# One Trainium2 core, attention plus routed experts: how the expert tokens reach TensorE transposed

## The reference

```
x + attention(xn) + experts(xn)
logits = xn @ gate_w.T ; probs = softmax(logits) over 8 experts ; two best experts a token
h = gelu(w1[e] @ xn + b1[e])            # 512 hidden features
y = w2[e] @ h + b2[e]                   # 128 features
experts(xn) = sum over the two choices of prob * y
```

## Time and profile before

| | us |
|---|---|
| three runs | 724.34, 726.56, 726.74 (median 726.56) |
| span of the profiled execution, first to last instruction | 724.1 |
| the profiled execution's own time beside its span | none is given by the profile |
| PE / DVE / ACT / POOL busy | 663.7 / 650.1 / 531.9 / 514.5 |
| expert stage, first product of tile 2 to that of tile 70 | 307.45 to 502.62 |

### The profile page before, as it was taken

How to read it: one execution, slowest core, us unless ns; L and a number is a source line. 1 busy time by engine, 2 the same in 40 slices (tenths; PEclk the granted TensorE clock), 3 DMA queues, 4 the chain that set the end, 5 groups by cost and what they waited for, 6 DMA issues and landing times.

```text
span 724.1 us, 25378 instructions
## 1 busy us (share of the span) xinstructions
PE 663.7 (92%) x8084; PEld 448.1 (62%) x8084; DVE 650.1 (90%) x1177; ACT 531.9 (73%) x1123; POOL 514.5 (71%) x613
## 2 busy tenths in 40 slices
PE   0377899999999999799999999999999999999996
PEld 0263445555555555599999999999455555555554
DVE  8989989999999999699999999999899999898991
ACT  2593388888888888667767767777787787787885
POOL 8680477777677656077777887787688888888782
PEclk9986799999999999999999999999999999999999
DMA  8859466776676676633333333332577777877652
GB/s 249 307 170 336 135 166 169 182 200 161 175 209 173 174 191 174 160 76 96 93 96 93 97 96 90 97 92 75 142 155 179 191 178 183 173 178 187 176 122 67
DMA packets 124919, 113.37 MB, mean 157 GB/s; under 512 B 16416, under 2 KB 112416, under 8 KB 124832
## 3 DMA queue, kind: packets, MB, share of 16 engines
q1 hardware_dynamic: 115600, 90.63, 47.7%
q0 software_dynamic: 8192, 16.86, 9.6%
q10 hardware_dynamic: 1040, 4.76, 1.8%
HBM read 64.72 MB, written 47.19 MB: 155 GB/s over the span
## 4 chain that ended last, share of the span: by engine, by line
PE 65%; DVE 13%; SPq 8%; DMA 6%; issue 5%; ACT 2%; ACTq 0%; DVEq 0%
PE bank L1266 13%; PE mx L1255 13%; PE bank L1135 12%; PE bank L1113 11%; PE mx L1147 7%; DVE mx L961 6%; DMA stack<-qk_dram 6%; PE bank L1033 2%; PE bank L1247 2%; PE bank L1195 2%; DVE A L796 2%; SPq L331 2%; PE bank L1157 1%; ACT A L715 1%; PE bank L1164 1%
## 5 line engine op out<-in xcount | busy, mean ns | idle before, releaser
L715 ACT ACTIVATE A<-bank 128x512 f32<-128x512 f32 x502 | 278.2, 597 | 63.8 <-PE bank L1135 55.8
L961 DVE TENSOR_REDUCE mx<-mx 128x4 f16<-128x1024 f32 x256 | 302.7, 1205 | 19.1 <-PE mx L1147 14.7
L1135 PE MATMUL bank<-stack 113*128 113x256 f16 x1004 | 170.4, 276 | 1.3 <-ACT A L715 0.8
L761 ACT ACTIVATE rows<-mx,b 128x256 f32<-128x256 f32 x284 | 120.1, 480 | 57.7 <-PE mx L1255 55.3
L556 POOL DMA_INDIRECT slots_x<-rows,pos x128 | 123.6, 966 | 51.8 <-PE bank L1135 32.0
L570 POOL TENSOR_SCALAR rows<-rows,slot_p 128x128 f32<-128x128 f32 x142 | 124.6, 887 | 43.9 <-DVE rows L1009 43.9
L607 POOL DMA_INDIRECT rows<-slots_y,pos x128 | 121.5, 950 | 37.5 <-issue 17.3
L1113 PE MATMUL bank<-A,V 128*32 128x256 f32 x2048 | 137.9, 387 | 1.7 <-ACT A L715 1.6
L1135 PEld LDWEIGHTS bank<-stack 113*128 113x128 f16 x1004 | 72.4, 97 | 89.4 <-ACT A L715 53.8
L1266 PE MATMUL bank<-w,rows 128*128 x1704 | 107.7, 219 | 0.6 <-DVE rows L1003 0.6
L1003 DVE TENSOR_TENSOR rows<-rows 128x512 f16<-128x512 f32 x142 | 101.4, 714 | 4.9
(11 more groups left out here) (145 smaller groups left out, 684.9 us busy)
## 6 DMA issues: line engine op xcount, KB each, us to landing
stack<-ctx_rest SPq DMA_DIRECT2D x64, 256.0 KB
stack<-qk_dram SPq DMA_DIRECT2D x128, 96.0 KB
rows<-slots_x SPq DMA_DIRECT2D x71, 129.0 KB, 2.3
slots_y<-rows SPq DMA_DIRECT2D x71, 128.0 KB, 1.8
qk_dram<-hi_qk SPq DMA_DIRECT2D x64, 128.0 KB
stack<-ctx_high SPq DMA_DIRECT2D x128, 64.0 KB
slots_x<-A ACTq DMA_DIRECT2D x1, 4644.0 KB, 20.3
w_stage<-in_w SPq DMA_DIRECT2D x8, 512.0 KB
```

Of the source, the lines that this page charges most:

```text
L715: act.activation(A[:, n % NA, :, :].rearrange("p h s -> p (h s)"), scores(k, n)[:, :], ACT.Exp, scale=SCALE).then_inc(s_xp, 1)
L761: act.activation(h32[r % 2][:, fc, :], bank[fc][:, 0:SLOT], ACT.Gelu_apprx_tanh, bias=b1[:, bass.ds(e + fc, 1)], scale=1 / FS).then_inc(s_ ...
L961: dve.tensor_reduce(mx[:, a, 8 * qt:8 * qt + 8].rearrange("q (i e w) -> q i e w", i=2, e=2)[:, :, g % 2], MX[u % 2][:, :].rearrange("q (i ...
L1135: mm = pe.matmul(scores(k, n)[:, i * S:(i + 1) * S], stack[0:SHIFT + 1, par, h, 1, c * P:(c + 1) * P], stack[0:SHIFT + 1, par, h, 0, :], s ...
```

## The change

It changes how a tile's tokens get from `slots_x` to TensorE and divides the two casts of the hidden values.

- `fetch(n)` is now two transfers on SP's queue: a transposing transfer of columns 2 to 257 of the tile's 256 rows straight into `xt[n % 4]`, and a small one of the first float32 of each row into `slot_p`. `xt` has four buffers, the raw buffers `xr` are gone. For n >= 4 both wait until all four groups of w1 of tile n-4 are done and until POOL has multiplied tile n-4.
- PE has no transposes in the stage, ACT no `turned_tokens`, POOL no copy of the probabilities. w1(t) waits for the transposing transfer of tile t.
- The cast of the hidden chunks 2 and 3 moves from DVE to ACT, behind the fourth Gelu of the same tile, whose completion it waits for. DVE's second subtraction waits for it (`s_fa`).

```diff
@@ buffers
-        xr32 = [carve(RW, F32).rearrange("p (s c) -> p s c", s=2) for _ in range(4)]
-        xr = [v.bitcast(F16) for v in xr32]
-        xt = [carve(2 * SLOT, F16).rearrange("p (a s) -> p a s", a=2) for _ in range(2)]
+        xt = [carve(2 * SLOT, F16).rearrange("p (a s) -> p a s", a=2) for _ in range(4)]
@@ SP
-            xs = slots_x.rearrange("(n s p) c -> n p s c", s=2, p=P)
+            xs = slots_x.bitcast(F16).rearrange("(n s) c -> n s c", s=SLOT)
+            ps = slots_x.rearrange("(n s p) c -> n p s c", s=2, p=P)
...
                 if n >= 4:
-                    sp.wait_ge(s_ft, n - 3)
-                    sp.wait_ge(s_sp, n - 3)
-                sp.dma_start(xr32[n % 4], xs[n]).then_inc(s_xr[n % 4], 16)
+                    sp.wait_ge(s_fu, 4 * (n - 3))
+                    sp.wait_ge(s_yp, n - 3)
+                sp.dma_start_transpose(xt[n % 4], xs[n][:, 2:RW]).then_inc(s_xr[n % 4], 16)
+                sp.dma_start(slot_p[:, n % 4, :].unsqueeze(2), ps[n][:, :, 0:1], allow_slow_non_contiguous=True).then_inc(s_sp[n % 4], 16)
@@ POOL
-                pool.wait_ge(s_sp, n + 1)
+                pool.wait_ge(s_sp[n % 4], 16 * (n // 4 + 1))
                 pool.wait_ge(s_fy, n + 1)
...
             for n in range(ET):
-                pool.wait_ge(s_xr[n % 4], 16 * (n // 4 + 1))
-                if n >= 4:
-                    pool.wait_ge(s_yp, n - 3)
-                pool.tensor_copy(slot_p[:, n % 4, :], xr32[n % 4][:, :, 0]).then_inc(s_sp, 1)
-                if n >= 3:
-                    weigh(n - 3)
-            for n in range(ET - 3, ET):
                 weigh(n)
@@ ACT
-            def turned_tokens(n):
-
-                act.wait_ge(s_ft, n + 1)
-                if n >= 2:
-                    act.wait_ge(s_fu, 4 * n - 4)
-                act.activation(xt[n % 2].rearrange("p a s -> p (a s)"), bank[4 + n % 2][:, 0:SLOT].bitcast(F16), ACT.Copy).then_inc(s_fx, 1)
...
                     for fc in range(FC):
-                        if fc == 2 and a:
-                            turned_tokens(t + 1)
                         act.wait_ge(s_fu, 4 * t + fc + 1)
                         act.activation(h32[r % 2][:, fc, :], ...Gelu_apprx_tanh...).then_inc(s_fg, 1)
+                    if t >= 2:
+                        act.wait_ge(s_fd, t - 1)
+                    act.wait_ge(s_fg, 4 * t + 4)
+                    act.activation(hp[r % 2][:, 0, 2:4, :], h32[r % 2][:, 2:4, :], ACT.Copy).then_inc(s_fa, 1)
@@ DVE
-                        dve.tensor_copy(hi, h).then_inc(s_fh, 1)
-                        dve.wait_ge(s_fh, 2 * t + hf + 1)
+                        if hf == 0:
+                            dve.tensor_copy(hi, h).then_inc(s_fh, 1)
+                            dve.wait_ge(s_fh, t + 1)
+                        else:
+                            dve.wait_ge(s_fa, t + 1)
                         dve.tensor_tensor(lo, h, hi, ALU.subtract).then_inc(s_fl, 1)
@@ PE
                 if a:
-                    ... (wait for the raw rows and for turned_tokens(t - 1))
-                    for part in range(2):
-                        for h in range(2):
-                            mm = pe.transpose(v[...], xr[r4][:, h, 2 + part * D:2 + (part + 1) * D], ident16[:, :])
-                    mm.then_inc(s_ft, 1)
                 if b:
-                    pe.wait_ge(s_fx, t + 1)
+                    pe.wait_ge(s_xr[r], 16 * (quad + 1))
...
-                            mm = pe.matmul(bank[fc][:, 0:SLOT], w1[...], xt[r % 2][:, pb, :], start=(n == 0), stop=(n == 2))
+                            mm = pe.matmul(bank[fc][:, 0:SLOT], w1[...], xt[r][:, pb, :], start=(n == 0), stop=(n == 2))
```

More of the change, by code:

```diff
@@ L269, in build @@
         s_xr = [sem(f"s_xr{i}") for i in range(4)]
-        s_ft, s_fx, s_fu, s_fg, s_fh, s_fl, s_fd, s_fy = (sem(n) for n in ("s_ft", "s_fx", "s_fu", "s_fg", "s_fh", "s_fl", "s_fd", "s_fy"))
-        s_sp, s_yp, s_both, s_sum = sem("s_sp"), sem("s_yp"), sem("s_both"), sem("s_sum")
+        s_sp = [sem(f"s_sp{i}") for i in range(4)]
+        s_fu, s_fg, s_fh, s_fa, s_fl, s_fd, s_fy = (sem(n) for n in ("s_fu", "s_fg", "s_fh", "s_fa", "s_fl", "s_fd", "s_fy"))
+        s_yp, s_both, s_sum = sem("s_yp"), sem("s_both"), sem("s_sum")
         s_ys = [sem(f"s_ys{i}") for i in range(4)]
@@ L691, in attend @@
                     g = u // 2
-                    if first_half and k == HALF and u == 2:
-                        turned_tokens(0)
                     if first_half and k == HALF and u in (0, 2):
@@ L1198, in attend @@
                         values(bo, paro, 3)
-                    if k == HALF and phase[0] == 0 and u == 2:
-                        pe.wait_ge(s_xp, 16 * HALF)
-                        expert_steps(expert, experts.of, -1, -1)
                     if u == 1 and opening:
@@ L1238, in expert @@
                 static = isinstance(t, int)
[L1239 to L1244, removed]
-                    for part in range(2):
-                        for h in range(2):
-                            mm = pe.transpose(v[:, part * SLOT + h * P:part * SLOT + (h + 1) * P], xr[r4][:, h, 2 + part * D:2 + (part + 1) * D], ident16[:, :])
-                    mm.then_inc(s_ft, 1)
                 if b:
-                    pe.wait_ge(s_fx, t + 1)
+                    pe.wait_ge(s_xr[r], 16 * (quad + 1))
                     for fc in range(FC):
@@ L1254, in expert @@
                         for n, (pa, pb) in enumerate(TERMS):
-                            mm = pe.matmul(bank[fc][:, 0:SLOT], w1[:, pa, bass.ds(e + fc * P, P)], xt[r % 2][:, pb, :], start=(n == 0), stop=(n == 2))
+                            mm = pe.matmul(bank[fc][:, 0:SLOT], w1[:, pa, bass.ds(e + fc * P, P)], xt[r][:, pb, :], start=(n == 0), stop=(n == 2))
                         mm.then_inc(s_fu, 1)
@@ L1275, in _ @@
             chosen.append(expert_steps(expert, experts.of, 2, ET - 1, chosen.pop()))
-            pe.wait_ge(s_fx, ET)
             phase[0] = 1
```

## The result

The changed kernel takes 746.56 us (743.35 to 749.99, 4 runs) against 726.57 (724.34 to 726.74, 4 runs): ratio 1.028, 95% interval 1.025 to 1.032. It is slower by 20 us. Forecast were 752, between 715 and 820. The profiled execution has a span of 741.6 and a time of 743.35, so 1.8 us lie around the span.

A forecast was written before the change was run, and what follows sets the result against it. PE bounds the expert stage, DVE second; after the change, a fetch wait would. Rounds of 9.8 us put tile 70 at 528.05 against 502.62, +25.4: span 724.1 to 749.5, plus 2.5 gives 752 us, range 715 to 820.

The forecast's parts named there:

- PE's own work: Expert stage: without the transposes, 0.22 us a tile, PE asks for 2.65 us instead of 2.87.
- The loop through POOL's multiplication: Expert stage: w1(t) to POOL's multiplication to the fetch to w1(t+3), 6.3 us + L per three tiles; 9.8 forecast.
- L: Expert stage: time from a transposing transfer's issue until it lands, taken as 3.5 us, between 2.2 and 5.2.
- The head: Start of the expert stage: w1(2) would start at about 305.3 us instead of 307.45.
- tile 0 has its tokens early enough: Start of the expert stage: fetches issued from 294.00 us land by 297.5, before w1(0) at 298.75.
- SP: Expert stage: the second transfer adds 0.42 us of issue a tile, 1.2 of 2.65 with the store, hidden.
- The DMA engines: Expert stage: 256 more small packets a tile, about 30 ns each, raise their share from 0.37 to about 0.55; hidden.
- would have been the limit: Expert stage: without moving one cast to ACT, DVE's 2.77 us a tile would exceed PE's 2.65.
- The clock: Expert stage: PE stays over 80% busy despite holes of 1.8 us in 9.8, so no clock loss is counted.
- The signs: Changed profile: PE holes of 1 to 2 us every third tile, busy near 80%; SP waits before fetch; landing near 3.5.
- Rivals 1 and 2: Expert stage: transposing lands like plain, 724 us (chance 0.12); or its own occupation sets the pace, about 885 us (0.15).
- Rival 3: Expert stage: POOL's multiplication speeds up to 1.35 us a pair, shortening the round by 0.43: 715 us, chance 0.13.

The follow-up runs named there:

- the repaired ones: Changed kernel with eight probability buffers, alone or with bias earlier, both casts on DVE, small transfer on ACT's queue: ratios 0.995, 0.986, 0.985, 0.982 to the kernel before.
- eight buffers: Changed kernel with eight instead of four buffers for the probabilities, a fetch waiting for POOL's multiplication of tile n-8: 797.97 us against 802.24 for the kernel before.
- the last of the experiments: Changed kernel with eight probability buffers, bias behind the first fetch, both casts on DVE, small transfer on ACT's queue: 794.12 us against 807.3 for the kernel before.

## Why the prediction was right, point by point

- PE's own work: 2.65 a tile without the transposes. Right, and reached to the last digit once nothing else was late.
- The loop through POOL's multiplication: right, in its place and its form. The 6.3 us from w1(t) to SP were 6.13 in the round shown and 6.04 in the mean; the handing over from the landed transfer to PE, 0.32 (344.06 to 344.38), I had left out, and in the mean PE starts 0.50 after the landing. With the plain transfer the same three terms are 6.01, 2.31 and 0.60, so that its round is 8.9 and not the 8.6 that the forecast has for a landing in 2.3.
- L: taken at 3.5, measured 2.62 median and 2.79 mean, 6 of 71 over 3.5. This is the term of the sum that was mis-sized: it was taken between the plain fetch and the slowest one, and the transfer stayed near the plain fetch. A round was forecast at 9.8 and took (521.89 - 316.09) / 22 = 9.355, 22 rounds 9.8 us less than forecast. The Trainium skill's page VectorE: DVE Perf Modes (The three transpose paths) has 1309 ns for one block, and four times that is not what this tile shows: four blocks land in 2.62, issue included. The Trainium skill's page Advanced Engine Details and Errata (X-Bar Transpose), by which transposing transfers are as fast as regular ones, is nearer: 2.62 against 2.34 for the plain fetch before, and 2.61 against 2.17 for the plain transfer in its place on one chip.
- The head: forecast as a gain of 2 us, w1(2) at 305.3. It was 309.82. The step that failed is "tile 0 has its tokens early enough": it has, but the eight issues of up to 1.5 us pushed b2 behind them, and DVE waited. Tile 4 began 3.6 us later than forecast. The two misses cancel in part: +3.6 - 9.8 = -6.2, tile 70 at 521.89 for 528.05. What follows it was 1.8 us shorter than before, and the profiled execution was the fastest of the four, so that the median came to 746.56 for 752. That it came so near is partly luck: the run with the bias earlier, whose tile 4 at 314.20 is nearer to the 312.45 of the forecast, took 741.95, 10 us under it.
- SP: hidden by my count, 1.2 us of 2.65 with plain issues. A transposing issue takes 1.19 and the small one 0.58, so SP has 2.24. In the changed kernel this still hid behind the loop for the most part; in the repaired ones it is what I put the remaining idle time down to.
- The DMA engines: a share of about 0.55 was forecast, and it was 0.40 between 350 and 400 us. The packets of 4 bytes take 9 ns each in the mean, not 30.
- DVE: "would have been the limit" without the moved cast. Wrong, with eight buffers: in the last of the experiments, with both casts on DVE, every step was 2.65, and DVE was busy 47.81 of 50 us, 2.53 a tile. The sum of means gave 2.77 where the earlier trace rows gives 46.61 of 50 at 2.870 a tile, 2.68, because instructions overlap; and the casts took 0.42 there instead of 0.46, for which no run shows a reason.
- The clock: counted at nothing, and 1.00 in the steady stage of this execution. In the head it fell, with PE idle for 4.94 us. At the end of the stage it fell to 0.50 for 3.4 us in both repetitions of the changed kernel and in the run with the bias earlier: in the first of these, PE had been busy 4.25 of the 6.80 us ahead of the fall, and the next step took 4.31 instead of 2.66, 1.65 us more.
- The signs: PE waits for the transfer in 24 places of 0.96 us in the mean, at every second or third tile, and SP waits for POOL ahead of the fetch (47.2 us) and little ahead of the store (8.4), both as said. PE is busy 87% of the stage and not 80%, and the landing is not near 3.5.
- Rivals 1 and 2: the plain transfer, landing in 2.29, gives 0.7 and 0.8% more than before and not "no change"; it removes a third of the excess and not more; the transposing transfer does not set the pace, since steps of 2.65 go with the same transfers. Rival 3: a quicker POOL did shorten the loop (a pair took 1.50 in the mean against 1.79), not down to the 1.35 it needed.

## What to carry to other kernels

When a transfer is moved from a raw buffer to the place where its data is used, write down what each buffer that it fills is released by, and follow the longest of these releases around to the next use: bytes that share a wait share its latest term, and a kilobyte of probabilities held up 128 KB of tokens here. Divide that round by the number of buffers and compare it with the bound engine's time for one step; more buffers for the small part, another queue for it and an earlier bias (with both casts on DVE again) took the time from 833.95 to 794.12 us on one chip, 4.8%. Count the issues on a queue by their own durations: the new kind took almost three times the plain one.

## What the runs showed of the hardware that I had not expected

- A transposing transfer of 256 rows of 512 bytes holds SP's queue for 1.19 us (plain: 0.42) but lands 1.40 us after its issue has ended (plain: 1.85), so that from start to landing the two differ by 0.3 us only (by 0.44 against a plain transfer of the same bytes in its place). The page counts 73216 packets under 512 bytes in place of 16416: 56800 more, 71 tiles of 800, the 256 small words among them.
- The 256 words of 4 bytes take 0.58 us to issue and land after 2.0, nearly as long as 128 KB.
- POOL's multiplication of 128x128 took 0.909 us in the mean beside two casts and two subtractions a tile on DVE, and 0.798 with one of the casts on ACT.
- One and the same program took 726 us on one chip and 802 and 807 on two others, with the expert stage alike and the attention longer (219.7 against 261.8 us for what follows tile 70). The runs do not show the cause.
